# A twelve-stage decoder in float32: a block-sparse ReLU layer by seven block products on token tile pairs, and identity products at places of every stage

## The chip, the cores and the metric

The kernel runs on one core of a Trainium2 chip. The metric is the device time of one execution in microseconds (us), lower is better. Five engines work beside each other, each with its own instruction stream: TensorE (PE in the profile) multiplies matrices and writes to the accumulating memory PSUM, VectorE (DVE), ScalarE (ACT) and GpSimd (POOL) do elementwise work, SyncE (SP) issues the transfers (DMAs). They order themselves by semaphores: an instruction adds to a counter when it has ended, and another engine waits until the counter has reached a number. An engine that waits holds up everything that stands behind the wait in its stream. TensorE's clock has two levels, 2.4 and 1.2 GHz; the profile gives the granted clock of a stretch as a share of the full one (PEclk).

## The reference

The input x has 16 x 64 tokens of 512 numbers, all in float32. Twelve layers follow each other, and each adds to x what it computes from the normalized x: `x = x + layer(layernorm(x), weights)`. The layers are named L0 to L3, each with a part attn, xattn and ffn. The one that is rewritten here is L1's ffn:

```python
inter = xf @ c1_w.T @ c2_w.T                   # 512 -> 16 -> 1792 scores
blk = inter.reshape(tokens, 1792 // 32, 32)
idx = argmax(blk, axis=-1) + arange(0, 1792, 32)   # one of each 32
h = relu(einsum('bkm,bm->bk', w1[idx], xf))    # hidden values of those alone
out = einsum('bk,bkm->bm', h, w2t[idx])
```

The other eleven (gated and attention layers with their own projections, softmaxes and tables) stay as they are in what they compute.

## The kernel before, in words

The 1024 tokens are T = 8 tiles of P = 128; x lies in SBUF throughout, as 128 x 8 x 512. Each layer is a stage with buffers and semaphores of its own (`Stage`, line 66); a barrier of all engines stands between two stages (`begin`, line 90). The stages run in the order l0a, l0x, l0f, l1a, l1x, l1f, l2a, l2x, l2f, l3a, l3x, l3f. Helpers hold what most stages share. `Front` (line 244) normalizes one tile on ACT (`norm`), turns it on TensorE by four products with the identity (`turn`, line 265) and copies it back out of PSUM (`copy`); at the end of a tile ACT copies the result out of PSUM (`out`) and POOL adds it to x (`residual`). `Ahead` measures mean and variance of x for the next stage while this one still runs. `Turned` (line 207, its `turns` at 227) turns all eight tiles at the start of l1x, l3a and l3x.

**l1f** (`stage_l1_ffn`, line 3171) takes one token tile at a time, in a written-out order on each engine. TensorE computes the 16 low values (`lowered`, line 3220), from them the scores of two chunks of 448 (`scores`), the hidden values for all 1792 columns in four chunks of 448 with K = 512 (`chunk`, line 3238), turns the hidden values in 14 blocks of 128 (`hidden_turn`, line 3247), and multiplies them by w2, 14 products of 512 columns (`out`, line 3259). DVE finds the first largest score of each 32 (line 3334 to 3348: largest, equal, times a falling ramp, largest, equal), and then takes the hidden value where it is largest and positive, and 0 elsewhere. ACT copies turned tiles out of PSUM. SP's queue brings the weights in this order: c1, c2, w1 in four column chunks (line 3210), w2. POOL has the additions to x and the roots of the norms alone. The profile counts two records of TensorE for each float32 product and one for each turned block of 128.

**The other places that the diff touches** are single spots of TensorE's streams: ahead of waits, between products, and at ends of stages. In `stage_bias` (l1x), `turns(n, h)` waits for the softmax'd scores before it turns them; `stage_gqa` builds l3a (`rope`) and l3x (`rms`), where `pair_sums` (line 1219) sums squares of queries and `scores` multiplies queries by keys; in `stage_l0_attn` TensorE begins with `context(g, 0)`, `turn(0, 0)` and `gate_up(0)` (24 records, line 2066); in `stage_l0_ffn` a tile's `zg` is turned for its last products (line 2523); `stage_small_attn` builds l1a (with `context`) and l2a; `stage_l2_ffn` has a chain of small steps per tile between TensorE and DVE; `stage_l3_ffn` is the last stage.

Each engine's order is written out by hand in these functions; no planner moves anything.

## Time and profile before

| | |
|---|---|
| time, median of 3 runs | 4074.86 us (4074.83 to 4080.53) |
| profiled execution, its own time | 4081.22 us |
| its span | 4079.4 us |
| TensorE busy / VectorE / ScalarE / GpSimd | 3819.3 / 2447.5 / 1403.4 / 696.3 us |
| mean granted TensorE clock | 0.966 of the full one |
| l1f, TensorE's first to last product | 1883.65 to 2128.9 us of the span |

A group line of the profile reads: line, engine, operation, out <- in, shapes, count | busy us, mean ns of one | idle time of the engine before them, and what ended most of it. A timeline line reads: start, duration, engine, line, work, number of records [idle before it <- what ended it]. A window line gives for a stretch the busy time of PE, PEld (loading of the stationary side, which overlaps PE), DVE, ACT and POOL with the number of instructions, then the granted clock, the DMA engines' share and GB/s.

### The profile page before, as it was taken

How to read it: one execution, taken by the hardware profiler on the slowest of the kernel's cores; microseconds unless marked ns; L12 is line 12 of the kernel's file. 1: busy time of each engine (PE TensorE's matmuls, PEld its weight loads, DVE VectorE, ACT ScalarE, POOL GpSimd, SP SyncE). 2: the span in 40 equal slices, each digit the busy share in tenths (PEclk: the TensorE clock that was granted, in tenths of full speed). 3: DMA queues.
4: the chain of work that ended last, by engine and by line, in shares of the span. 5: the costliest groups of instructions: out<-in, count | busy, mean ns of one | idle time of the engine just before them, and what ended most of it. 6: DMA issues, size and time to landing. Idle time of an engine off the chain costs nothing. (4 is left out here: it accounts for less than half of the span.)

```text
span 4079.4 us, 50937 instructions
## 1 busy us (share of the span) xinstructions
PE 3819.3 (94%) x18954; PEld 2130.2 (52%) x18954; DVE 2447.5 (60%) x4150; ACT 1403.4 (34%) x2522; POOL 696.3 (17%) x680
## 2 busy tenths in 40 slices
PE   8899989998989899999999889799999989999997
PEld 3343435554456477775447664345555545555564
DVE  0988955552247455555447658876766665565563
ACT  2988935552223211111113334211111133333232
POOL 1111111121001344441000111121211110000000
PEclk9999989999989899999999989899999999999998
DMA  5111121001100433311001022101001021111110
GB/s 191 54 37 52 51 72 34 32 29 61 41 35 14 174 114 115 129 53 75 1 29 41 1 105 60 66 2 41 22 21 42 1 69 37 37 37 37 42 37 24
DMA packets 133966, 215.40 MB, mean 53 GB/s; under 512 B 42576, under 2 KB 95056, under 8 KB 123104
## 3 DMA queue, kind: packets, MB, share of 16 engines
q1 hardware_dynamic: 133728, 212.19, 14.9%
q8 instruction: 154, 2.52, 0.2%
q14 instruction: 84, 0.69, 0.1%
HBM read 168.12 MB, written 44.04 MB: 52 GB/s over the span
## 5 line engine op out<-in xcount | busy, mean ns | idle before, releaser
L1320 PE MATMUL l3a_po<-l3a_wo,l3a_cT 128*128 128x512 f32 x512 | 231.2, 600 | 1.2 <-ACT l3a_cT L1517 1.2
L1320 PEld LDWEIGHTS l3a_po<-l3a_wo,l3a_cT 128*128 128x128 f32 x512 | 96.2, 191 | 121.0 <-issue 116.6
L830 DVE TENSOR_TENSOR x<-x,l1x_po 128x512 f32<-128x512 f32 (+1 forms) x154 | 88.3, 581 | 89.0 <-PE l1x_po L622 88.2
L1208 PE MATMUL l3x_pj<-kvT,l3x_ws 128*128 128x512 f32 x256 | 121.6, 607 | 2.3 <-DVE l3x_qT L1647 2.2
L1208 PE MATMUL l3a_pj<-kvT,l3a_ws 128*128 128x512 f32 x256 | 120.7, 605 | 1.5 <-ACT l3a_saves L1459 0.8
L2796 POOL TENSOR_TENSOR l0x_q<-l0x_q,l0x_qi 128x512 f32<-128x512 f32 x64 | 65.3, 1042 | 303.6 <-DVE l0x_qi L3084 303.6
L1320 PE MATMUL l3x_po<-l3x_wo,l3x_cT 128*128 128x512 f32 x256 | 115.3, 593 | 0.7 <-ACT l3x_cT L1517 0.7
L1320 PE MATMUL l3x_pc<-l3x_wo,l3x_cT 128*128 128x512 f32 x256 | 115.2, 593 | 0.0
L1105 POOL TENSOR_TENSOR l3x_ws<-l3x_wq 128x256 f32<-128x256 f32 x16 | 13.8, 860 | 579.5 <-DMA l3x_wo<-in_L_xattn_Wo 377.6
L2349 DVE TENSOR_SCALAR_CACHE_REDUCE l0a_keep<-l0a_keep,l0a_scalars 128x1376 uint16<-128x1376 uint16 x64 | 105.4, 1646 | 3.6 <-DVE l0a_scalars L2355 1.5
L1614 DVE TENSOR_TENSOR l3a_part<-l3a_raw,l3a_sinq 64x512 f32<-64x512 f32 x128 | 102.2, 799 | 4.0
L3267 PE MATMUL l1f_po<-l1f_w,l1f_hT 128*128 128x512 f32 x224 | 101.6, 599 | 1.9 <-ACT l1f_hT L3310 1.9
L3243 PE MATMUL l1f_ph<-l1f_w,l1f_xT 128*128 128x448 f32 x256 | 103.4, 552 | 0.0
L723 ACT COPY l1x_cT<-l1x_pa 128x512 f32<-128x512 f32 x64 | 34.4, 589 | 197.9 <-PE l1x_pa L614 197.9
L2349 DVE TENSOR_SCALAR_CACHE_REDUCE l0a_keep<-l0a_a,l0a_scalars 128x1376 uint16<-128x1376 uint16 x60 | 98.8, 1646 | 3.8 <-DVE l0a_scalars L2355 1.3
L2212 ACT ACTIVATE l0a_signs<-l0a_lowest_a,l0a_scalars 128x1376 uint16<-128x1376 uint16 x68 | 97.9, 1440 | 6.4 <-DVE l0a_lowest_a L2364 5.3
L622 PE MATMUL l1x_po<-l1x_wo,l1x_cT 128*128 128x256 f32 x376 | 97.2, 381 | 1.2 <-issue 1.2
L1459 ACT COPY l3a_saves<-l3a_pj 128x512 f32<-128x512 f32 x48 | 28.0, 582 | 199.1 <-PE l3a_pj L1208 173.0
L2660 DVE COPY l0x_fill_kv<-l0x_fill 128x512 f32<-128x512 f32 x33 | 22.8, 691 | 120.7 <-PE l0x_fill L2646 62.6
L580 PE MATMUL l1x_pj<-l1x_folds,l1x_ws 128*128 128x512 f32 x192 | 93.7, 614 | 1.5 <-DVE l1x_qT L786 1.5
L194 POOL TENSOR_TENSOR norm_rstd<-norm_half,minus_half 128x1 f32<-128x1 f32 x70 | 41.1, 596 | 315.3 <-DVE norm_half L189 315.3
L1208 PE MATMUL l3x_pj<-kvT,l3x_wq 128*128 128x512 f32 x192 | 90.5, 600 | 3.6 <-DVE l3x_qT L1647 2.3
(591 smaller groups left out, 8898.5 us busy)
## 6 DMA issues: line engine op xcount, KB each, us to landing
l1x_kb<-l1x_keys SPq DMA_DIRECT2D x32, 512.0 KB, 4.7
l1x_vb<-l1x_values SPq DMA_DIRECT2D x32, 512.0 KB, 3.4
l1x_keys<-l0a_kv SPq DMA_DIRECT2D x40, 256.0 KB, 2.0
...
```

Of the source, the lines that this page charges most:

```text
L194: self.nc.gpsimd.tensor_tensor(self.rstd[:, t:t + 1], self.half[:, t:t + 1], self.m.minus_half[:, 0:1], ALU.pow).then_inc(self.root_ready, 1)
L580: mm = pe.matmul(pj[:, p if k % 2 else 1 - p, :], weights, stream, start=c == 0 and not more_of_bank, stop=c == 1, skip_group_check=more_o ...
L622: mm = pe.matmul(bank, rows[:, c], cols[:, c], start=opens and c == 0, stop=c == 1, skip_group_check=not opens)
L830: nc.vector.tensor_tensor(dst, dst, src, ALU.add).then_inc(added, 1)
L1208: mm = pe.matmul(pj[:, p if k % 2 else 1 - p, :], weights, stream, start=c == 0, stop=c == 1)
L1320: mm = pe.matmul(outs[t % 2][:, :], cT[:, h, t * P:(t + 1) * P], wo[:, u, h, :], start=h == 0, stop=h == GH - 1)
L1614: nc.vector.tensor_tensor(batches(part[low:low + S, 1, :]), batches(src[high:high + S]), s, ALU.mult).then_inc(link, chain.next())
L2212: ins = nc.scalar.activation(signs[:, :], words, ACT.Sign, bias=at[:, :], scale=-1.0, accum_out=total[:, :])
L2349: nc.vector.tensor_scalar(below, words, found[:, :], 0.0, ALU.is_lt, ALU.add, accum_out=cnt[:, :]).then_inc(link, step.next())
L2796: nc.gpsimd.tensor_tensor(qv, qv, qi[:, c % 2, b, :].unsqueeze(2).to_broadcast([P, XH, XD]), ALU.mult).then_inc(q_done, 1)
L3243: mm = pe.matmul(ph[:, c % 2, 0:CH1], f.xT[:, u, k, :], w1[:, k, c * CH1:(c + 1) * CH1], start=k == 0, stop=k == KC - 1)
L3267: mm = pe.matmul(f.po[:, :], hT[:, j, :], w2[:, j, :], start=j == 0, stop=j == HC1 - 1)
```

## The change

**First**, a helper issues identity products, which write to a PSUM bank that nobody reads at that time, and whose result is not used:

```diff
+def spin(pe, m, bank, count):
+
+    for _ in range(count):
+        pe.matmul(bank[:, 0:P], m.ident[:, :], m.ident[:, :], start=True, stop=True)
 
 
```

It is called in all stages. The number of products that are executed is 426 as the calls and their loops add up: l0a 25, l0x 42, l0f 30, l1a 34, l1x 39, l1f 26, l2a 48, l2x 24, l2f 72, l3a 33, l3x 44, l3f 9. Most calls stand ahead of a wait, some (at the ends of stages) behind the last product. Where such a call stands ahead of a wait for one engine, the other wait, which guards the bank, is moved ahead of it. Four of the places (l0f; l3x; l3a; `closing` of l3a and l3x), and l1a, where the turn of tile 2 is moved behind the turns of tile 0:

```diff
+                    if n >= T - 2:
+                        pe.wait_ge(zT_ready, n + 1)
+                        spin(pe, m, f.pt, 8 if n == T - 2 else 15)
                     pe.wait_ge(zg_ready, n + 2)
-                    pe.wait_ge(f.xT_ready, n + 3 if not last(n) else n + 2)
                     for k in range(KC):
...
+                        if n == 0 and p == 0:
+                            spin(pe, m, po, 20)
                         pe.wait_ge(q_squared, square_q(n, p) + 2)
...
+                    if rope and hn == 2:
+                        spin(pe, m, px[:, 1], 30)
                     if rope:
...
+                    if rms:
+                        pe.wait_ge(pj_copied, unit_v(GROUPS - 1, NV - 1) + 2)
+                        spin(pe, m, pj[:, 0], 14)
                     turns(GROUPS - 1, 3)
                     attend(GROUPS - 1, 0)
                     rest_of_out(GROUPS - 1, 1)
+                    spin(pe, m, px[:, 0], 3)
 
                 over_groups(opening, group, closing)
...
                 def body(n, u):
                     if within(n + 1):
                         project(n + 1, 1 - u)
-                    if within(n + 2):
+                    if within(n + 2) and not (context and n == 0):
...
@@ -4491,8 +5008,19 @@
                         rotate(n + 1)
                     if n == T - 1:
                         product(n)
+                        spin(pe, m, f.pt, 4)
+                    if context and n == 0:
+                        spin(pe, m, f.pt, 9)
                     turns(n, 0)
+                    if n == T - 1:
+                        spin(pe, m, f.pt, 5)
+                    if context and n == 0:
+                        spin(pe, m, f.pt, 5)
                     turns(n, 1)
+                    if context and n == 0:
+                        f.turn(pe, 2)
+                    if n == T - 1:
+                        spin(pe, m, f.pt, 4)
```

In l0a it is one call of 18 ahead of `gate_up(0)`, in l2f 3 in each tile's round and 5 in each round of the next loop:

```diff
+                    spin(pe, m, f.po, 3)
                     pe.wait_ge(f.xT_ready, n + 2)
                     pe.wait_ge(l_read, n + 1)
                     for k in range(KC):
                         mm = pe.matmul(py[:, 0:ZP], f.xT[:, u, k, :], w[:, k, :], start=k == 0, stop=k == KC - 1)
                     mm.then_inc(l_ready, 1)
 
+                spin(pe, m, f.po, 4)
                 f.turn(pe, 0)
+                spin(pe, m, f.po, 4)
                 pe.wait_ge(loaded, 64)
                 over_tiles(pe, body)
```

**Second**, l1f takes token tiles in pairs p of 0 to 3. The up product of a pair and half the columns (j = 2p + q, q the half) is a product of a 2 x 2 block matrix of x (two tiles by two halves of K) and one of w1 (two halves of K by two chunks of 448 columns), and is computed by seven block products in place of eight, from sums of blocks: four sums of x per pair, four of w1 per half once. The down product has 2 x 2 blocks of h (two tiles by two halves of 896) and of w2 (by two halves of 256 columns), with four sums of h per pair and four of w2 once. All these sums are POOL's:

```diff
+                def mix_x(p, i):
+
+                    u = p % 2
+                    one, two, one2, two2 = x_block(u, 0, 0), x_block(u, 0, 1), x_block(u, 1, 0), x_block(u, 1, 1)
+                    if i == 1:
+                        pool.wait_ge(pt_copied, x_at(p, 1) + 2)
+                        if p >= 2:
+                            pool.wait_ge(up_ready, up_at(2 * p - 3, 7) + 1)
+                        nc.gpsimd.tensor_tensor(xs[:, u, 0], one2, two2, ALU.add).then_inc(x_mixed, 1)
+                    elif i == 2:
+                        pool.wait_ge(x_mixed, 4 * p + 2)
+                        nc.gpsimd.tensor_tensor(xs[:, u, 1], xs[:, u, 0], one, ALU.subtract).then_inc(x_mixed, 1)
+                    elif i == 3:
+                        nc.gpsimd.tensor_tensor(xs[:, u, 2], one, one2, ALU.subtract).then_inc(x_mixed, 1)
+                    else:
+                        pool.wait_ge(x_mixed, 4 * p + 3)
+                        nc.gpsimd.tensor_tensor(xs[:, u, 3], two, xs[:, u, 1], ALU.subtract).then_inc(x_mixed, 1)
...
+                def mix_up(q, i):
+
+                    if i == 1:
+                        pool.wait_ge(w1_loaded[2 * q], 16)
+                        pool.wait_ge(w1_loaded[2 * q + 1], 16)
+                        nc.gpsimd.tensor_tensor(w1s[:, q, 0], up_block(q, 0, 1), up_block(q, 0, 0), ALU.subtract).then_inc(up_mixed, 1)
+                    elif i == 2:
+                        pool.wait_ge(up_mixed, 4 * q + 2)
+                        nc.gpsimd.tensor_tensor(w1s[:, q, 1], up_block(q, 1, 1), w1s[:, q, 0], ALU.subtract).then_inc(up_mixed, 1)
+                    elif i == 3:
+                        nc.gpsimd.tensor_tensor(up_block(q, 0, 1), up_block(q, 1, 1), up_block(q, 0, 1), ALU.subtract).then_inc(up_mixed, 1)
+                    else:
+                        pool.wait_ge(up_mixed, 4 * q + 3)
+                        nc.gpsimd.tensor_tensor(w1s[:, q, 2], up_block(q, 1, 0), w1s[:, q, 1], ALU.subtract).then_inc(up_mixed, 1)
+
+                def mix_down():
+
+                    low_, high = down_block(0, 1), down_block(1, 1)
+                    pool.wait_ge(down_loaded, 16)
+                    nc.gpsimd.tensor_tensor(w2s[:, 0], high, low_, ALU.subtract).then_inc(down_mixed, 1)
+                    pool.wait_ge(down_mixed, 2)
+                    nc.gpsimd.tensor_tensor(low_, low_, down_block(0, 0), ALU.subtract).then_inc(down_mixed, 1)
+                    pool.wait_ge(down_mixed, 3)
+                    nc.gpsimd.tensor_tensor(w2s[:, 1], high, low_, ALU.subtract).then_inc(down_mixed, 1)
+                    pool.wait_ge(down_mixed, 4)
+                    nc.gpsimd.tensor_tensor(w2s[:, 2], down_block(1, 0), w2s[:, 1], ALU.subtract).then_inc(down_mixed, 1)
+                def mix_hidden(p):
+
+                    one, two, one2, two2 = h_block(0, 0), h_block(0, 1), h_block(1, 0), h_block(1, 1)
+                    pool.wait_ge(pt_copied, turn_at(2 * p, 1, 1) + 2)
+                    if p:
+                        pool.wait_ge(down_ready, down_at(p - 1, 7) + 1)
+                    nc.gpsimd.tensor_tensor(hs[:, 0], one, one2, ALU.subtract).then_inc(h_mixed, 1)
+                    pool.wait_ge(pt_copied, turn_at(2 * p + 1, 1, 1) + 2)
+                    pool.wait_ge(h_mixed, sum_at(p, 3) + 1)
+                    nc.gpsimd.tensor_tensor(one2, one2, two2, ALU.add).then_inc(h_mixed, 1)
+                    pool.wait_ge(h_mixed, sum_at(p, 1) + 1)
+                    nc.gpsimd.tensor_tensor(hs[:, 1], one2, one, ALU.subtract).then_inc(h_mixed, 1)
+                    pool.wait_ge(pt_copied, turn_at(2 * p + 1, 0, 1) + 2)
+                    pool.wait_ge(h_mixed, sum_at(p, 2) + 1)
+                    nc.gpsimd.tensor_tensor(hs[:, 2], two, hs[:, 1], ALU.subtract).then_inc(h_mixed, 1)
+
                 f.roots(pool)
-                f.residual(pool, ahead)
+                mix_x(0, 1)
+                mix_up(0, 1)
+                mix_x(0, 2)
+                mix_up(0, 2)
+                mix_x(0, 3)
+                mix_up(0, 3)
+                mix_up(0, 4)
+                mix_x(0, 4)
+                mix_up(1, 1)
+                mix_up(1, 2)
+                mix_up(1, 3)
+                mix_up(1, 4)
+                for i in (1, 2, 3, 4):
+                    mix_x(1, i)
+                mix_down()
+                mix_hidden(0)
+                for p in range(1, T // 2):
+                    if p < T // 2 - 1:
+                        for i in (1, 2, 3, 4):
+                            mix_x(p + 1, i)
+                    mix_hidden(p)
+                    for t in (2 * p - 2, 2 * p - 1):
+                        ahead.root(pool, t, t)
+                ahead.root(pool, T - 2, T - 2)
 
             @block.tensor
```

The seven up products of a j are of two products of 448 columns each, and `down(p, k)` is of seven products of 256 columns. Several of the seven end in one PSUM bank, one after another, and are taken out in between: ACT copies the bank to h four times per j (`save`), DVE adds another bank to it (`join`), and the ReLU now reads h from SBUF in place of PSUM:

```diff
+                    bank = ph[:, {1: 0, 2: 1, 3: 2, 4: 0, 5: 0, 6: 0, 7: 2}[k], 0:CH1]
+                    opens = k in (1, 2, 3)
+                    for c in range(2):
+                        mm = pe.matmul(bank, rows[:, c], cols[:, c], start=opens and c == 0, stop=c == 1, skip_group_check=not opens)
+                    mm.then_inc(up_ready, 1)
+
...
+                    bank = {1: po[:, 0, 0:MID], 2: po[:, 1, 0:MID], 3: po[:, 1, MID:D], 4: po[:, 0, 0:MID],
+                            5: po[:, 1, MID:D], 6: po[:, 1, 0:MID], 7: po[:, 0, 0:MID]}[k]
+                    opens = k in (1, 2, 3, 6)
+                    for c in range(HALF):
+                        mm = pe.matmul(bank, rows[:, c], cols[:, c], start=opens and c == 0, stop=c == HALF - 1, skip_group_check=not opens)
+                    mm.then_inc(down_ready, 1)
...
+                def save(j, what):
+
+                    s, c = {"m1": (0, 0), "u2": (0, 1), "u3": (1, 1), "21": (1, 0)}[what]
+                    act.wait_ge(up_ready, up_at(j, {"m1": 1, "u2": 4, "u3": 5, "21": 6}[what]) + 1)
+                    if j >= 2:
+                        act.wait_ge(pt_filled, turn_at(j - 2, s, 1) + 2)
+                    nc.scalar.copy(hidden(j, s, c), ph[:, 0, 0:CH1]).then_inc(saved, 1)
...
+                def join(j, block):
+
+                    s, c = int(block[0]) - 1, int(block[1]) - 1
+                    dve.wait_ge(up_ready, up_at(j, {"11": 2, "22": 3, "12": 7}[block]) + 1)
+                    dve.wait_ge(saved, saved_at(j, {"11": "m1", "22": "u3", "12": "u2"}[block]) + 1)
+                    nc.vector.tensor_tensor(hidden(j, s, c), hidden(j, s, c), ph[:, 2 if c else 1, 0:CH1], ALU.add).then_inc(joined, 1)
+
+                def relu(j, s):
+
+                    dve.wait_ge(joined, join_at(j, "22" if s else "12") + 1)
+                    if s:
+                        dve.wait_ge(saved, saved_at(j, "21") + 1)
+                    dve.wait_ge(link, hit_at(j, s, 1) + 6)
+                    for c in range(2):
+                        nc.vector.scalar_tensor_tensor(hidden(j, s, c), hidden(j, s, c), 0.0, hits[:, s, c, :],
+                                                       ALU.max, ALU.mult).then_inc(h_ready, 1)
+
```

The additions to x are DVE's, from PSUM, five per pair (256 or 512 columns); ACT's copy and POOL's addition of before are gone. `lowered` is computed once per pair, for 256 tokens. TensorE's order is written out for pairs; the even round, and its beginning and end:

```diff
+                def even(j):
+
+                    p = (j - 4) // 2
+                    hidden_turn(j - 2, 0, 0)
+                    up(j, 1)
+                    scores(j, 1)
+                    hidden_turn(j - 2, 0, 1)
+                    down(p, 5)
+                    hidden_turn(j - 2, 1, 0)
+                    up(j, 2)
+                    hidden_turn(j - 2, 1, 1)
+                    up(j, 3)
+                    down(p, 6)
+                    up(j, 4)
+                    scores(j, 0)
+                    up(j, 5)
+                    down(p, 7)
+                    up(j, 6)
+                    up(j, 7)
...
+                spin(pe, m, pt, 5)
+                turn(0, 0)
+                spin(pe, m, po[:, 0], 6)
+                turn(0, 1)
+                spin(pe, m, po[:, 0], 4)
+                lowered(0)
+                spin(pe, m, po[:, 0], 3)
+                scores(0, 1)
+                for k in (1, 2, 3):
+                    up(0, k)
+                scores(0, 0)
+                for k in (4, 5, 6, 7):
+                    up(0, k)
+                up(1, 1)
...
+                for k in (3, 4, 5, 6, 7):
+                    down(p + 1, k)
+                spin(pe, m, pt, 8)
```

The norm and the turn of x, the first-largest search and the order of the loads are as before; one PSUM bank serves all turned blocks and the low values.

## Rows read from the trace of the kernel before

**Rows 1.** The page: the span and each engine's busy time.

```profile
span 4079.4 us, 50937 instructions
PE 3819.3 (94%) x18954; PEld 2130.2 (52%) x18954; DVE 2447.5 (60%) x4150; ACT 1403.4 (34%) x2522; POOL 696.3 (17%) x680
```

**Rows 2.** Windows of l1f: start:end; length, busy us per engine (instructions), PEclk, DMA share, GB/s.

```profile
1884.00:2131.00 247.00, 241.75 (x752) 118.09 (x750) 124.39 (x215) 32.68 (x63) 14.00 (x16) 0.98 0.08 31
1950.00:1980.00 30.00, 29.76 (x96) 14.59 (x94) 15.62 (x27) 4.17 (x8) 1.77 (x2) 1.00 0.00 1
```

**Rows 3.** Timeline of PE over one token tile of l1f: start, duration, work.

```profile
1950.36 1.02 PE L3235 MATMUL l1f_pi<-l1f_wc,l1f_low 16*128 16x448 f32 x4
...
1980.38 1.02 PE L3235 MATMUL l1f_pi<-l1f_wc,l1f_low 16*128 16x448 f32 x4
```

**Rows 4.** Timeline of PE in l1f's first token tile.

```profile
1902.43 3.17 PE L3243 MATMUL l1f_ph<-l1f_w,l1f_xT 128*128 128x448 f32 x8
1905.44 3.60 PE L3267 MATMUL l1f_po<-l1f_w,l1f_hT 128*128 128x512 f32 x8
1908.87 1.04 PE L3256 MATMUL l1f_pt<-ident,l1f_h 128*128 128x128 f32 x8
```

**Rows 5.** Timeline of PE at the end of l1x: products of 256 columns.

```profile
1876.78 1.03 PE L622 MATMUL l1x_po<-l1x_wo,l1x_cT 128*128 128x256 f32 x4
1877.64 1.03 PE L622 MATMUL l1x_pj<-l1x_wos,l1x_cs 128*128 128x256 f32 x4
```

**Rows 6.** Groups by form, POOL, whole span: work count | busy us, mean ns | idle before.

```profile
L476 POOL TENSOR_TENSOR l1x_ws<-l1x_wq 128x256 f32<-128x256 f32 x16 | 11.8, 740 | 0.0
L1108 POOL TENSOR_TENSOR l3x_ws<-l3x_wq 128x256 f32<-128x256 f32 x16 | 20.4, 1274 | 0.0
L482 POOL TENSOR_TENSOR l1x_sbias<-l1x_sbias,l1x_mask 128x2048 f32<-128x2048 f32 x8 | 36.2, 4521 | 8.0 <-DVE l1x_mask L775 8.0
```

**Rows 7.** Line 3210, the loads of l1f's up weights.

```profile
DMA to landing us min/median/max: 6.1/8.6/10.9
```

**Rows 8.** Groups by form, l1f, DVE.

```profile
L3348 DVE TENSOR_TENSOR l1f_hit<-l1f_rank,l1f_first 128x448 f32<-128x448 f32 x32 | 20.0, 625 | 1.1
```

**Rows 9.** Windows of other stages, columns as in rows 2.

```profile
580.00:610.00 30.00, 24.02 (x89) 8.54 (x90) 19.32 (x24) 12.30 (x22) 8.17 (x8) 0.83 0.09 26
1122.00:1150.00 28.00, 20.00 (x44) 8.59 (x42) 6.26 (x26) 3.21 (x8) 2.32 (x3) 0.76 0.03 10
1180.00:1200.00 20.00, 17.18 (x162) 14.56 (x164) 15.94 (x17) 7.87 (x13) 0.00 (x0) 0.66 0.05 14
1320.00:1336.00 16.00, 10.91 (x40) 5.35 (x40) 3.66 (x7) 3.68 (x5) 1.46 (x2) 0.68 0.06 17
1372.00:1388.00 16.00, 14.26 (x84) 9.01 (x84) 5.71 (x10) 3.85 (x7) 0.00 (x0) 0.68 0.20 67
2672.00:2688.00 16.00, 8.83 (x47) 5.38 (x48) 13.46 (x20) 1.80 (x3) 3.12 (x3) 0.68 0.01 1
2131.00:2162.00 31.00, 20.95 (x185) 18.69 (x186) 10.45 (x16) 5.72 (x10) 1.04 (x2) 0.67 0.58 228
2380.00:2416.00 36.00, 28.20 (x107) 23.15 (x107) 10.17 (x38) 14.47 (x26) 6.33 (x15) 0.53 0.74 295
4032.00:4048.00 16.00, 8.51 (x21) 4.52 (x22) 0.22 (x1) 3.41 (x5) 0.00 (x0) 0.57 0.06 18
```

**Rows 10.** Timeline of PE: gaps in l0f and l3a, [idle before it <-releaser].

```profile
1141.99 1.12 PE L2523 MATMUL l0f_pt<-ident,l0f_zg 128*128 128x128 f32 x4 [4.08 <-DVE l0f_zg L2599]
...
2679.17 1.97 PE L1273 MATMUL l3a_pS<-l3a_kT,l3a_qT 128*64 128x64 f32 x32 [8.74 <-DVE l3a_qT L1617]
```

**Rows 11.** Timeline of PE at new places in l0a and l3x.

```profile
41.85 9.47 PE L2066 MATMUL l0a_pg<-l0a_wg,l0a_xT 128*128 128x512 f32 x24 [0.83 <-ACT l0a_xT L270]
...
3298.44 1.06 PE L1230 MATMUL l3x_pc<-l3x_qsq,l3x_ones 128*32 128x512 f32 x8
3299.44 3.84 PE L1156 MATMUL l3x_pj<-l3x_wv,kvT 128*128 128x128 f32 x32
```

577 lines of the change are left out of this document (443 added, 134 removed).

## The prediction

> **What bounds the kernel now.** I read the page first: TensorE is busy 3819.3 of 4079.4 us, no other engine above 60% [rows 1]. So a change pays where it takes away TensorE's work or lets it run at the higher clock. Then the windows of l1f, the stage that is rewritten: over the stage TensorE is busy 241.8 of 247 us, and in a steady tile 29.76 of 30.00 us, beside 15.6 us of VectorE, 4.2 of ScalarE and 1.8 of GpSimd [rows 2]. The timeline shows the same: a tile starts at 1950.36 and the next at 1980.38, 30.0 us of back to back products [rows 3]. l1f is bound by TensorE alone, and eight tiles of it make 240 us. Last come windows in the other stages, where PEclk lies at 0.53 to 0.83 [rows 9]: there TensorE computes at half clock for a part of the time, after gaps in which it waited [rows 10].
>
> **l1f, TensorE's products.** Eight records of 448 columns take 1905.44 - 1902.43 = 3.01 us, 0.376 each; eight of 512 take 1908.87 - 1905.44 = 3.43 us, 0.429 each [rows 4]. Four records of 256 columns take 0.86 us, 0.215 each [rows 5]: half as wide is half as long, so nothing is lost on the narrower down products. A pair of tiles had 64 up records, 24.1 us, and 56 down records, 24.0 us. It gets 7 x 2 x 2 x 2 = 56 up records, 21.1 us, and 7 x 7 x 2 = 98 of 256 columns, 21.1 us. That is 5.9 us per pair, **-23.8 us** in four.
>
> **l1f, what else TensorE gains.** The low product once per pair, and 0.24 us of waits per tile [rows 2] that two PSUM users less could save: about 0.5 us per pair, -2. The stage's clock of 0.98 over 247 us is at most 5 us lost [rows 2], all at its beginning; the 18 identity products there should give back half, -2.4.
>
> **l1f, what the other engines get.** GpSimd's price for a sum of two tiles: 0.74 us for 256 columns, 4.52 for 2048 [rows 6]; on the line between them 896 columns cost 2.1 us and 1792 cost 4.0. A second row has 256 columns at 1.27 us, in l3x, beside a busier VectorE [rows 6]; that is a factor of 1.7 and my upper price. Per pair GpSimd gets 4 x 0.74 + 4 x 2.1 = 11.4 us (19 at the upper price), of a pair's 54 us. VectorE has 31.2 us per pair, gets six joins of 448 columns near 0.63 [rows 8] and five additions, about 38 to 41 us in all. ScalarE loses two copies, gets eight, about 12. None becomes the bound, and the written-out order puts other products between a bank's fill and its next use; cover for a copy of 0.6 us is a product of 1.5 us (4 x 0.376). If that cover were gone, four copies per j over eight j would cost up to 8 x 4 x 0.6 = 19 us. One wait I do see: at j = 4 the scores wait for VectorE's search of the half before, +2.
>
> **The opening of l1f** is where it pays. A load of w1 lands 8.6 us after issue in the median and 10.9 at most [rows 7], so the second slice is there near 1892, and GpSimd's first sum of w1 can't start before. The four sums of w1 and four of x that j = 0 needs take 4 x 2.1 + 4 x 0.74 = 11.4 us, to 1903.5; at the upper price 19 us, to 1911. TensorE, from about 1890 with 28 records of 0.376 = 10.5 us, would be through near 1900.5. So it waits 3 to 11 us, then perhaps again for the sums of the second half (8.4 us more on GpSimd, for 10.5 us of products). Bounds 3 and 14; I take **+7**, nearer to the cheap price since VectorE is no busier here than in l1x. The sums of w2 (4 x 4.0 = 16, or 27 us) end between 1931 and 1955, and are needed near 1947: hidden by the products of j = 1 and 2, at the upper price up to 8 us late.
>
> The Trainium skill's page "SBUF — State Buffer", section "SBUF: two separate sides", says that a VectorE operation with two SBUF inputs and a GpSimd operation that reads SBUF exclude each other for their whole length. By that rule GpSimd's sums wait for VectorE's search and ReLU, and VectorE for the sums; the trace's 1.27 beside 0.74 agrees with it in kind. By the rule VectorE would stand at up to 41 + 11 = 52 us of the pair's 54, still no bound in the steady part.
>
> **At l1f's end** VectorE adds half tiles straight from PSUM where ScalarE's copy and GpSimd's addition stood; the eight identity products take about what this saves. Sum for l1f: -23.8 - 2 - 2.4 + 7 + 2 = **-19** (from -27 to -4).
>
> **The identity products' price.** One is two records of 128 columns: half of a pair of 256-column records is 0.215 us; by the 32 records of 3.84 us [rows 11] it is 0.24. 426 of them are 92 to 102 us, the double at half clock. In a gap they cost nothing: 15 of them are 3.2 us in a gap of 4.08, 30 are 6.5 in 8.74 [rows 10]. At half clock they would be 6.4 and 12.9, and so 2 and 4 us late. Two places have no gap. In l0a 18 products, 3.9 us, stand ahead of records that waited 0.83 us: +3.0. In l3x 20 products, 4.3 us, stand ahead of line 1230, which followed at 3298.44 with no idle time in front of it: +4.3 [rows 11]. With 0.7 at l1f's end, **+8**. In l2f 62 stand beside VectorE's chain of small steps; I cost them at nothing because VectorE sets that pace; uncovered they are 13 us. The moved waits guard banks that are copied long before, and l1a's turn of tile 2, moved behind the turns of tile 0, has a tile's products before it is needed: nothing for both.
>
> **What the clock gives back.** A stretch with a clock share c has lost at most (1 - c) times its length, if TensorE was busy throughout. Six windows within stages (the first six of [rows 9]) lose 5.1, 6.7, 6.8, 5.1, 5.1 and 5.1 us, and three more of the same kind about 3.4 each: 44 us. TensorE is busy 95 of the 126 us in the six, three quarters, so 33 is what can come back: **-33**. The three stage starts (the last of [rows 9]) lose 10.2, 16.9 and 6.9 us, three more 3.4 each, also 44 us. There TensorE waits for loads (DMA share 0.58 and 0.74) and for norms, which no clock makes faster. Bounds 0 and 30 (its busy share of 0.69); I take **-12**.
>
> **The sum.** -19 - 33 - 12 + 8 = -56 against the profiled execution's own 4081.2 us: 4025. That execution lies 6.4 us above the median shown, with one of the three runs beside it and two at 4074.8; I carry that over: 4019, and say 4020. A measurement of this kernel can tell about 0.2%, 8 us, from no change.
>
> **The rivals.**
> - *The sums are in the way* (B). GpSimd's sums at the upper price or worse, and ScalarE's copies between the products of one bank, eat what the seventh product saves: l1f gives nothing, the clock as forecast. 4081.2 - 37 - 6.4 = 4038. For it: 1.27 us, and up(4), up(5), up(6) all in one bank. Against it: TensorE is the only busy engine.
> - *The clock falls elsewhere* (C). Identity products bridge a gap, but what comes after them is as thin as before, and the clock falls in the next gap; they also run at half clock and end late. Clock gain 0, +8 in the way, l1f -19: 4070, less 6.4: 4064. For it: in four of the six windows TensorE is busy 0.55 to 0.80 of the time. Against it: the windows with a clock of 1.00 have gaps as well, only smaller ones.
> - *Everything works* (D). l1f -27, -44 within the stages, -30 at starts, +8: 4081 - 93 - 6.4 = 3982.
> - *Slower* (E). The identity products stand in front of work that was ready: their places are after a semaphore that comes later than I read it, in l2f, l2a, l1a and at ends. With half of the 92 us in the way and no clock returned it is +46 - 19 = +27, 4102; with all of it 4147. It decides from 19 us in the way, a fifth of the products, with no clock gained. Against it: the gaps of 2 to 9 us are in the trace just where the large calls stand.
> - *It doesn't do what it says* (F): TensorE's clock does not respond to such products and they fit all gaps; with B together, 4075, no change.
>
> **The numbers.** Forecast 0.63, B 0.13, C 0.11, D 0.07, E 0.04, F 0.02. The range takes the forecast's own bounds (l1f 8 either way, in-stage clock 11, starts 12 to 18, added as unlike errors: about 25), reaches over B and towards C and D, and leaves out E, F, most of C and part of D: 3994 to 4056. Faster is all but E and F, 0.94; same 0.02, slower 0.04.
>
> **What would show it.** In the changed kernel: l1f's pair period 54 us in place of 60, TensorE busy all through it, with idle time in its first 25 us put down to GpSimd; VectorE near 40 us per pair. The six windows at a PEclk above 0.9. l0a and l3x some 3 and 4 us longer at the two places. Wrong I would be if idle time stands between the up products of a j in the steady part (B), or if the clock of the six windows stays below 0.8 (C).

## The result, and the profile after

The changed kernel takes 4038.3 us (median of 4 runs, 4035.5 to 4046.2) against 4076.3 us (4 runs, 4074.8 to 4080.5): ratio 0.9913, 95% interval 0.9899 to 0.9927. That is 35 to 38 us less, clear of the 0.2% that can be told, inside the range of 3994 to 4056, and some two thirds of the 56 us forecast. The profiled execution is again a late one of its kernel, 4046.2 us, with a mean granted clock of 0.984 in place of 0.966.

The page, span and busy times:

```profile
span 4044.3 us, 52994 instructions
PE 3842.6 (95%) x19910; PEld 2222.6 (55%) x19910; DVE 2504.3 (62%) x4194; ACT 1416.9 (35%) x2542; POOL 770.5 (19%) x716
```

TensorE is busy 23 us longer than in [rows 1] although the span is 35 us shorter: the identity products count as busy. Taken between the first real products of two stages, as the timeline of TensorE gives them, the stages are as follows (us; l3f from the turning of its weights on; the last two columns are experiments told below):

| stage | before | changed | without the two | small sums |
|---|---|---|---|---|
| l0a | 548.3 | 551.8 | 548.7 | 547.7 |
| l0x | 440.6 | 436.9 | 436.9 | 436.9 |
| l0f | 154.7 | 149.7 | 148.9 | 148.9 |
| l1a | 185.9 | 180.5 | 177.3 | 177.4 |
| l1x | 544.0 | 537.7 | 537.7 | 537.7 |
| **l1f** | 251.4 | 242.4 | 242.4 | 232.9 |
| l2a | 186.9 | 185.9 | 180.9 | 180.5 |
| l2x | 63.3 | 61.3 | 61.8 | 62.1 |
| l2f | 235.5 | 231.4 | 228.9 | 228.8 |
| l3a | 647.3 | 647.7 | 647.2 | 646.9 |
| l3x | 759.7 | 759.3 | 756.7 | 756.5 |
| l3f | 51.7 | 49.6 | 49.7 | 49.8 |

l1f gives 9.0 of its 19 us, and the eleven others 26 together.

**The clock.** Windows of the changed kernel (start:end; length, busy us and instructions of PE, PEld, DVE, ACT, POOL, then PEclk, DMA share, GB/s). The first nine stand at or near the work of the nine windows in [rows 9], moved as the stages are (in the same order); then all of l1a and l1f's beginning:

```profile
580.00:610.00 30.00, 27.89 (x152) 13.93 (x149) 22.05 (x27) 12.91 (x24) 8.18 (x8) 1.00 0.12 36
1122.00:1150.00 28.00, 23.24 (x109) 13.94 (x109) 7.29 (x29) 4.22 (x9) 4.33 (x6) 0.98 0.04 13
1170.00:1190.00 20.00, 16.94 (x185) 14.97 (x185) 15.60 (x16) 8.43 (x14) 0.00 (x0) 0.83 0.06 15
1310.00:1326.00 16.00, 13.76 (x91) 8.87 (x86) 6.86 (x13) 4.39 (x6) 3.08 (x4) 1.00 0.06 17
1355.00:1375.00 20.00, 17.89 (x141) 11.23 (x140) 10.76 (x15) 5.17 (x9) 3.80 (x3) 1.00 0.19 65
2640.00:2656.00 16.00, 14.02 (x88) 9.15 (x87) 14.43 (x22) 1.80 (x3) 1.95 (x2) 0.89 0.01 2
2106.00:2137.00 31.00, 25.75 (x264) 24.14 (x266) 10.50 (x17) 5.73 (x10) 1.08 (x2) 0.89 0.57 228
2352.00:2388.00 36.00, 30.23 (x187) 23.22 (x187) 13.31 (x47) 14.66 (x26) 5.69 (x14) 0.95 0.73 296
3997.00:4013.00 16.00, 9.30 (x39) 7.09 (x38) 1.24 (x8) 4.22 (x7) 0.00 (x0) 0.68 0.07 19
1149.00:1329.00 180.00, 168.03 (x1650) 117.47 (x1646) 116.96 (x135) 67.42 (x105) 19.35 (x18) 0.97 0.09 28
1867.00:1920.00 53.00, 42.20 (x143) 20.52 (x142) 45.20 (x45) 11.63 (x21) 40.91 (x21) 0.90 0.36 142
```

Within the stages 0.83, 0.76, 0.66, 0.68, 0.68 and 0.68 have become 1.00, 0.98, 0.83, 1.00, 1.00 and 0.89, and at the stage starts 0.67, 0.53 and 0.57 are 0.89, 0.95 and 0.68. The forecast asked for above 0.9 within the stages: four of six. l1f's beginning is at 0.90, with gaps of its own. A clock share is not yet time: 0.966 over 4079.4 us is 139 us of full clock lost, 0.984 over 4044.3 us is 65, so 74 us of it came back, and the kernel is 35 us shorter, 9 of them by l1f.

**l1f.** Its steady part first, scores of one half at the same place of two successive pairs on TensorE's timeline (start, duration, work):

```profile
1981.24 1.02 PE L3426 MATMUL l1f_pi<-l1f_wc,l1f_low 16*128 16x448 f32 x4
...
2034.02 1.02 PE L3426 MATMUL l1f_pi<-l1f_wc,l1f_low 16*128 16x448 f32 x4
```

A pair takes 2034.02 - 1981.24 = 52.8 us where two tiles took 60.0 [rows 3]; 54 was forecast. VectorE is busy 40.0 us of it, as forecast, and TensorE all of it. Four pairs at this pace would save 29 us. So some 20 us are lost elsewhere in the stage, and the idle gaps in TensorE's timeline (in brackets, with what ended them) say where:

```profile
1881.93 1.25 PE L3426 MATMUL l1f_pi<-l1f_wc,l1f_low 16*128 16x448 f32 x4 [3.26 <-DVE l1f_hits L3743]
1886.93 1.77 PE L3474 MATMUL l1f_ph<-l1f_w,l1f_xs 128*128 128x448 f32 x4 [0.62 <-ACT l1f_h L3672]
...
1913.45 3.36 PE L3474 MATMUL l1f_ph<-l1f_w,l1f_xs 128*128 128x448 f32 x4 [4.92 <-DVE l1f_h L3759]
...
1922.10 1.77 PE L3474 MATMUL l1f_ph<-l1f_w1s,l1f_xs 128*128 128x448 f32 x4 [1.05 <-DVE l1f_h L3759]
...
1966.80 1.02 PE L3426 MATMUL l1f_pi<-l1f_wc,l1f_low 16*128 16x448 f32 x4 [2.05 <-DVE l1f_hits L3743]
```

There are ten gaps of 0.55 us or more between the stage's first scores and its last products, 14.9 us together, eight of them in the first 65 us. The four longest end with VectorE (3.3, 4.9, 1.1 and 2.1 us); the others are 0.55 to 0.62 us each, mostly for ScalarE's copy between two products of one bank, where the written order of the first halves has nothing to put in between. VectorE's groups in l1f (line, operation, count | busy, mean ns | idle before):

```profile
L3751 DVE TENSOR_TENSOR l1f_hits<-l1f_rank,l1f_first 128x448 f32<-128x448 f32 x32 | 35.5, 1110 | 1.1
L3746 DVE TENSOR_TENSOR l1f_rank<-l1f_hits,ramp 128x448 f32<-128x448 f32 x32 | 35.2, 1099 | 1.1
L3743 DVE TENSOR_TENSOR l1f_hits<-l1f_pi,l1f_best 128x448 f32<-128x448 f32 x32 | 20.0, 624 | 1.1
L3759 DVE TENSOR_TENSOR l1f_h<-l1f_h,l1f_ph 128x448 f32<-128x448 f32 x24 | 14.7, 613 | 2.1 <-PE l1f_ph L3474 1.7 <-ACT l1f_h L3672 0.3
```

These four kinds of pass over 448 columns have the same size, and two cost 1.1 us in place of 0.62 in [rows 8]. They are the two whose inputs both lie in SBUF: the other two read PSUM as well. The ReLU (L3768) has both inputs in SBUF too, and stays at 0.65 us in the mean and 1.15 at most: in this run it hardly ever falls beside a sum. Their single instructions on the timeline of VectorE:

```profile
1904.12 4.45 DVE L3746 TENSOR_TENSOR l1f_rank<-l1f_hits,ramp 128x448 f32<-128x448 f32 x1
1908.61 0.62 DVE L3749 TENSOR_REDUCE l1f_first<-l1f_rank 128x14 f32<-128x448 f32 x1
1909.26 3.61 DVE L3751 TENSOR_TENSOR l1f_hits<-l1f_rank,l1f_first 128x448 f32<-128x448 f32 x1
...
1914.63 2.55 DVE L3746 TENSOR_TENSOR l1f_rank<-l1f_hits,ramp 128x448 f32<-128x448 f32 x1
```

and at the same time on GpSimd's, the sums of w2:

```profile
1904.13 3.96 POOL L3346 TENSOR_TENSOR l1f_w2s<-l1f_w 128x1792 f32<-128x1792 f32 x1
1908.17 4.22 POOL L3348 TENSOR_TENSOR l1f_w<-l1f_w 128x1792 f32<-128x1792 f32 x1
1912.47 4.23 POOL L3350 TENSOR_TENSOR l1f_w2s<-l1f_w 128x1792 f32<-128x1792 f32 x1
```

The rank of 1904.12 ends at 1908.57, 0.5 us after the sum that began at 1904.13 has ended at 1908.09; the mark of 1909.26 ends at 1912.87, again 0.5 us after the next sum. So each step looks as if it waited for a whole sum; whether it does, and with which inputs, is tested below. Over the four sums of w2 VectorE's four ranks and marks took some 12 us more than their 0.62 each, and TensorE stood behind it.

### The profile page after: what moved, and what is told of

Its sections match the earlier page's. It is cut to its first block and busy times, and to the rows that moved or that the text cites. A ratio compares the mean times of both kernels' runs of the same rounds, so it can differ in the third digit from the quotient of the medians.

```text
span 4044.3 us, 52994 instructions
## 1 busy us (share of the span) xinstructions
PE 3842.6 (95%) x19910; PEld 2222.6 (55%) x19910; DVE 2504.3 (62%) x4194; ACT 1416.9 (35%) x2542; POOL 770.5 (19%) x716
## 5 line engine op out<-in xcount | busy, mean ns | idle before, releaser
L2234 ACT ACTIVATE l0a_signs<-l0a_a,l0a_scalars 128x1376 uint16<-128x1376 uint16 x64 | 92.5, 1445 | 1.1
L1220 PE MATMUL l3a_pj<-kvT,l3a_wq 128*128 128x512 f32 x192 | 88.4, 596 | 4.2 <-DMA l3a_wo<-in_L_attn_Wo 2.2
```

The costliest lines, as they stand in the source:

```text
L1220: mm = pe.matmul(pj[:, p if k % 2 else 1 - p, :], weights, stream, start=c == 0, stop=c == 1)
L2234: ins = nc.scalar.activation(signs[:, :], words, ACT.Sign, bias=at[:, :], scale=-1.0, accum_out=total[:, :])
```

## The experiments

All runs are compared with the kernel before, run beside them on the same chip; "less" and "more" of a stage are read from the timelines as in the table.

**The two parts, one at a time.** The first run leaves all identity products out:

```diff
 def spin(pe, m, bank, count):
-    for _ in range(count):
-        pe.matmul(bank[:, 0:P], m.ident[:, :], m.ident[:, :], start=True, stop=True)
+    return
```

> The changed kernel with every identity product left out, so that only the seven-product l1f and the moved waits are new. The theory (two parts that add up): in the changed kernel's trace l1f is 9.0 us shorter from its first product to the next stage's, with its own identity products at the start worth about 2 of that; so 7 us less than before, about 4069 us (4065 to 4072), the mean clock back at 0.966, and VectorE's marks and ranks in l1f again up to 4.4 us long in place of 0.62. Rival (l1f gives its forecast 19 us once no identity product stands in its way): 4057.

Measured: 4071.7 us, ratio 0.9987 (0.9977 to 0.9997). l1f takes 248.1 us, 3.3 less than before and not 7. Two windows of its beginning, and two gaps on TensorE's timeline:

```profile
1880.00:1920.00 40.00, 33.30 (x92) 14.82 (x92) 28.90 (x41) 8.49 (x16) 25.78 (x18) 0.83 0.49 191
1920.00:1970.00 50.00, 42.23 (x138) 22.85 (x137) 39.16 (x44) 10.93 (x20) 27.45 (x11) 0.86 0.00 0
```

```profile
1933.44 2.33 PE L3473 MATMUL l1f_ph<-l1f_w1s,l1f_xs 128*128 128x448 f32 x4 [3.81 <-DVE l1f_h L3758]
1941.45 1.86 PE L3425 MATMUL l1f_pi<-l1f_wc,l1f_low 16*128 16x448 f32 x4 [2.72 <-DVE l1f_hits L3742]
```

The waits of 3.8 and 2.7 us are the same kind as above, and the clock is at 0.83 and 0.86 over 90 us. l1f is 5.7 us longer than with its own identity products, not the 2.4 of the forecast. One more stage moved here: l1x takes 539.6 us with no identity product in it, 4.4 less than before. Whether its moved wait or chance in the clock does that is open. The second run has l1f of before (its function put back as it was) and everything else of the change:

```diff
 def stage_l1_ffn(nc, m, w_c1, w_c2, w_1, w_2):
-    HALF, MID = HC1 // 2, D // 2
...
+        f = Front(nc, st, m)
```

> The old l1f beside all identity products of the other stages. The theory: the eleven other stages are 27 us shorter in the changed kernel's trace (spans between first products of the stages), so 4076 - 27 = 4049 us (4045 to 4053), mean clock about 0.983. Rival (the new l1f's dense products are what keeps the clock for the stages behind it): l2a and l2x lose 3 us or more, 4053 or above.

Measured: 4047.7 us, ratio 0.9940 (0.9924 to 0.9957). So by the ratios the identity products of the other stages bring 24 us, the new l1f alone 5, and the whole change 35, each known to within 4 to 7 us. The 6 us between are what the identity products in l1f itself bring there (242.4 us against 248.1), but the intervals alone would allow for none. l2a and l2x lose nothing (179.6 and 61.6 us); the rival falls. l1f takes 253.6 us, 2.2 more than before, with its code unchanged; no run shows why.

**The two places in the way:**

```diff
-                spin(pe, m, f.po, 18)
                 gate_up(0)
...
-                        if n == 0 and p == 0:
-                            spin(pe, m, po, 20)
                         pe.wait_ge(q_squared, square_q(n, p) + 2)
```

> The changed kernel without the 18 identity products ahead of gate_up(0) in l0a and the 20 ahead of the first pair_sums in l3x. The theory (they stand in front of work that was ready and give no clock back): l0a 3.5 us and l3x 4 us shorter, 4031 us (4028 to 4034) against 4038. Rival (they keep the clock high in what follows): a stretch at half clock appears behind one of the two places and the time is 4036 or more.

Measured: 4029.9 us, ratio 0.9890 (0.9873 to 0.9906) against 0.9913 (0.9899 to 0.9927); the intervals overlap, and the two stages have to decide. In the changed kernel they stood as two runs of records on TensorE:

```profile
40.78 4.18 PE L60 MATMUL l0a_po<-ident 128*128 128x128 f32 x36
...
3264.88 4.73 PE L60 MATMUL l3x_po<-ident 128*128 128x128 f32 x40
3269.54 1.06 PE L1244 MATMUL l3x_pc<-l3x_qsq,l3x_ones 128*32 128x512 f32 x8
```

4.2 and 4.7 us long, and line 1244 follows at once. Without them the first one's place shows

```profile
42.09 9.47 PE L2084 MATMUL l0a_pg<-l0a_wg,l0a_xT 128*128 128x512 f32 x24 [0.85 <-ACT l0a_xT L277]
```

a gap of 0.85 us, as before. l0a is 3.1 us shorter and l3x 2.6, 5.7 of the 8 us by the medians, and no new stretch at half clock appears behind either. Over all profiles l3x takes 759.3 to 760.6 us with these products and 756.3 to 758.3 without, l0a 549.3 to 552.0 and 546.6 to 548.7, so the two costs hold. The two profiles differ by 17 us, and most of the rest looks like chance: l1a, whose code is the same in both, is 3.2 us shorter, l2a 5.0 and l2f 2.5. For l1a

```profile
1145.00:1322.00 177.00, 165.02 (x1650) 114.58 (x1646) 117.11 (x135) 67.14 (x105) 19.29 (x18) 0.99 0.09 29
```

the clock is 0.99 where the changed kernel's trace has 0.97 over the same work; in all eleven other profiles with identity products it took 177.3 to 177.5 us. The changed kernel's own profile caught the clock low there and in l2a; together these are 8 us, as much as it lies above its median.

**Turns in place of products:**

```diff
-    for _ in range(count):
-        pe.matmul(bank[:, 0:P], m.ident[:, :], m.ident[:, :], start=True, stop=True)
+    for _ in range(2 * count):
+        pe.transpose(bank[:, 0:P], m.ident[:, :], m.ident[:, :])
```

> Each identity product is replaced by two turns of the identity in TensorE's transpose mode, so about the same time on TensorE and the same places. Theory one (any occupation of TensorE holds its clock): mean clock 0.984, 4038 us (4034 to 4042). Theory two (the Trainium skill, page TensorE: Matmul & The Clock Gate, Part 4: PE-mode transpose, says that a transpose does not count as busy in the same way): the mean clock falls back to near 0.966 while the time in the way stays, 4065 us or more.

Measured: 4045.6 us, ratio 0.9926 (0.9910 to 0.9943), not to be told from the change's 0.9913. The clock and two windows:

```profile
core 0: 4046.0 us, clock 0.984
```

```profile
580.00:610.00 30.00, 27.65 (x151) 13.21 (x146) 21.72 (x27) 12.57 (x22) 8.17 (x8) 1.00 0.12 36
2640.00:2656.00 16.00, 13.87 (x94) 9.67 (x93) 14.50 (x22) 1.80 (x3) 2.88 (x3) 0.89 0.01 2
```

0.984, and 1.00 and 0.89 in the windows, as with real products, and most stages take what they take with products (l0x 436.9, l1a 177.3, l2x 61.3 us). So in these stages a float32 turn in transpose mode holds the clock as a product does, and theory two falls; the time lies somewhat above the 4034 to 4042 us of theory one. The exception is l1f: it takes 250.6 us, 8 more than in the change, at a granted clock of 0.94, as low as in the run without any identity product and not 0.97. Whether the turns or chance did that is open.

**GpSimd's sums and VectorE.** First, the twelve sums of weight blocks are left out, and then the four of w2 alone. Of the first:

```diff
-                        nc.gpsimd.tensor_tensor(w1s[:, q, 0], up_block(q, 0, 1), up_block(q, 0, 0), ALU.subtract).then_inc(up_mixed, 1)
+                        nc.gpsimd.tensor_tensor(thin[:, 4 * q + 0:4 * q + 1], m.ident[:, 0:1], m.ident[:, 0:1], ALU.subtract).then_inc(up_mixed, 1)
...
-                        rows, cols = xs[:, u, 0], w1s[:, q, 0]
+                        rows, cols = xs[:, u, 0], up_block(q, 0, 0)
```

> The changed kernel, but GpSimd's sums of weight blocks (eight of w1, four of w2) are left out: in their place it adds one column each, with the same semaphores, and TensorE reads plain blocks of the same size, so the output is not the reference's. The theory (these sums hold VectorE's operations with two SBUF inputs back, and VectorE holds TensorE): VectorE's marks and ranks fall to 0.62 us near l1f's start, the idle time of TensorE in front of up products and scores there (3.3, 4.9, 1.1 us and more) goes but for the copies' 0.6 each, and l1f is 10 to 14 us shorter: 4026 us (4022 to 4031). Rival (the opening is bound by the loads and by ScalarE's copies between products of one bank): at most 4 us shorter, 4034 or above.

and of the second, which changes w2's sums and their readers alone:

```diff
-                    nc.gpsimd.tensor_tensor(w2s[:, 0], high, low_, ALU.subtract).then_inc(down_mixed, 1)
+                    nc.gpsimd.tensor_tensor(thin[:, 0:1], m.ident[:, 0:1], m.ident[:, 0:1], ALU.subtract).then_inc(down_mixed, 1)
...
-                        rows, cols = hs[:, 1], w2s[:, 1]
+                        rows, cols = hs[:, 1], down_block(0, 0)
```

> The same for the four sums of w2 alone; the eight of w1 stay. The theory: TensorE's 4.9 and 1.1 us in front of products at 1913 and 1922 us, while VectorE's rank and mark took 4.4 and 3.6 us beside sums of 4 us each, go: l1f 5 to 7 us shorter, 4032 us (4029 to 4036). Rival (what counts are the sums of w1 in the opening, the later ones are hidden): 4037 or above.

Measured: 4022.1 us, ratio 0.9870 (0.9854 to 0.9887), with l1f at 227.8 us, 14.6 less; and 4029.0 us, ratio 0.9888 (0.9869 to 0.9907), with l1f at 234.4, 8.0 less. So the sums cost l1f 14.6 us, 8.0 of them those of w2, which the prediction had hidden. TensorE's gaps without any weight sum:

```profile
1874.06 1.02 PE L3428 MATMUL l1f_pi<-l1f_wc,l1f_low 16*128 16x448 f32 x4 [0.81 <-DVE l1f_hits L3745]
1877.40 1.77 PE L3476 MATMUL l1f_ph<-l1f_w,l1f_xs 128*128 128x448 f32 x4 [0.62 <-ACT l1f_h L3674]
...
1948.44 1.02 PE L3428 MATMUL l1f_pi<-l1f_wc,l1f_low 16*128 16x448 f32 x4 [2.05 <-DVE l1f_hits L3745]
```

The wait of 3.3 us is 0.8, the copies' 0.6 are still there and so is the one of 2 us at j = 4; those of 4.9 and 1.1 us are gone. All gaps that are left in l1f come to 5.9 us: 2.1 at j = 4, the rest ScalarE's copies and 0.8 for VectorE.

The gaps of 14.9 us have become 5.9, which is 9.0 of the 14.6. The rest is the clock. Windows over l1f of the changed kernel, without w2's sums, and without any weight sum:

```profile
1866.00:2108.00 242.00, 225.25 (x917) 146.69 (x916) 180.30 (x265) 45.41 (x85) 88.27 (x53) 0.97 0.08 32
1858.00:2092.00 234.00, 223.68 (x917) 145.63 (x916) 169.00 (x265) 45.31 (x85) 72.33 (x54) 0.98 0.09 34
1861.00:2089.00 228.00, 220.28 (x922) 145.04 (x922) 160.63 (x265) 45.65 (x85) 56.36 (x54) 1.00 0.09 36
```

0.97, 0.98 and 1.00: by these shares some 7, 5 and 0 us are lost to the clock. w2's sums cost 6.4 us of gaps (8.5 are left without them) and some 2 of clock; w1's cost 2.6 us of gaps and some 5 of clock, which falls behind the gap of 3.4 us in front of the second scores.

That shows that the sums do it, not how. The next run leaves all sums in place, and takes away the second SBUF input of VectorE's steps:

```diff
-                    nc.vector.tensor_tensor(blocks(mask), score, best[:, :].unsqueeze(2).to_broadcast(wide),
+                    nc.vector.tensor_tensor(score, score, best[:, :].unsqueeze(2).to_broadcast(wide),
                                             ALU.is_equal).then_inc(link, 1)
                     dve.wait_ge(link, done + 3)
-                    nc.vector.tensor_tensor(blocks(rank[:, :]), blocks(mask), m.ramp[:, :].unsqueeze(1).to_broadcast(wide),
+                    nc.vector.tensor_tensor(score, score, m.ramp[:, :].unsqueeze(1).to_broadcast(wide),
                                             ALU.mult).then_inc(link, 1)
...
-                        pe.wait_ge(link, hit_at(j, 1, 1) + 3)
+                        pe.wait_ge(link, hit_at(j, 1, 1) + 6)
```

> The changed kernel, but VectorE keeps marks and ranks of the search in the scores' own PSUM bank, so that none of its five steps has two SBUF inputs; the next scores of TensorE wait for the whole search and not for its first two steps. GpSimd's sums are all there. The theory (an exclusive lock between a VectorE operation with two SBUF inputs and a GpSimd operation, not a shared bandwidth): VectorE's five steps take 0.62 us each also beside the sums, l1f is 4 to 9 us shorter, 4031 us (4028 to 4035); the longer wait for the scores gives some of it back in the steady part. Rival (any VectorE operation is slowed by GpSimd's sums, or the other way): steps of more than 1 us stay, no gain, 4038 or above.

Measured: 4045.0 us, ratio 0.9928 (0.9912 to 0.9945): no gain. But the step itself (durations in ns, least/median/most, of 32):

```profile
L3745 DVE TENSOR_TENSOR l1f_pi<-l1f_pi,ramp x32: 632/632/633, 1867.4 to 2071.5; 128x448 f32<-128x448 f32 x32
```

never takes more than 633 ns, beside all the same sums of up to 4.2 us. What waits now is the ReLU, whose inputs are both in SBUF; on VectorE's timeline

```profile
1904.58 0.63 DVE L3745 TENSOR_TENSOR l1f_pi<-l1f_pi,ramp 128x448 f32<-128x448 f32 x1
...
1906.98 8.27 DVE L3767 SCALAR_TENSOR_TENSOR l1f_h<-l1f_h,l1f_hits 128x448 f32<-128x448 f32 x2
```

two of them take 8.3 us in place of 1.15, one sum of w2 each. And the longer wait that the edit adds for the next scores shows on TensorE:

```profile
1919.11 1.86 PE L3425 MATMUL l1f_pi<-l1f_wc,l1f_low 16*128 16x448 f32 x4 [6.63 <-DVE l1f_hits L3750]
...
1964.68 1.02 PE L3425 MATMUL l1f_pi<-l1f_wc,l1f_low 16*128 16x448 f32 x4 [4.06 <-DVE l1f_hits L3750]
```

6.6 and 4.1 us. GpSimd is freed as well: its 256-column sums of x take 1.1 us in seven of 16 cases in the changed kernel and 0.73 in 14 of 16 here. So the steps came out as the theory has it and not as the rival, while the time came out as the rival's: the cure is not one. l1f takes 250.7 us, 8 more, 3.5 of them gaps and most of the rest clock (0.95 in place of 0.97). The same with the first scores moved and without the two places:

```diff
-                for k in (1, 2, 3):
+                for k in (1, 2, 3, 4, 5):
                     up(0, k)
                 scores(0, 0)
-                for k in (4, 5, 6, 7):
+                for k in (6, 7):
                     up(0, k)
```

> Both: marks and ranks in PSUM, the first scores(0, 0) moved behind up(0, 5), and without the identity products ahead of gate_up(0) in l0a and of the first pair_sums in l3x. The theory: gains of the two add up, 8 and 7 us: 4022 us (4018 to 4027). Rival (l1f's beginning is bound by the sums themselves once VectorE is free): l1f only 4 us shorter, 4027 to 4031.

Measured: 4037.2 us, ratio 0.9914 (0.9895 to 0.9933), outside the forecast and its rival. That is 8 us below the run before, about what the two places are worth, and l1f is no better (249.9 us).

If one waits for the other's whole instruction, then short instructions are the cure:

```diff
+                def sums(n, dst, a, b, op, sem):
+                    for c in range(n):
+                        last_ = nc.gpsimd.tensor_tensor(dst[:, c], a[:, c], b[:, c], op)
+                    last_.then_inc(sem, 1)
...
-                        nc.gpsimd.tensor_tensor(w1s[:, q, 0], up_block(q, 0, 1), up_block(q, 0, 0), ALU.subtract).then_inc(up_mixed, 1)
+                        sums(2, w1s[:, q, 0], up_block(q, 0, 1), up_block(q, 0, 0), ALU.subtract, up_mixed)
...
-                    nc.gpsimd.tensor_tensor(w2s[:, 0], high, low_, ALU.subtract).then_inc(down_mixed, 1)
+                    sums(HALF, w2s[:, 0], high, low_, ALU.subtract, down_mixed)
```

> The kernel without the two (e3_without_two), and GpSimd makes each sum of w1 in two pieces of 448 columns and each of w2 in seven of 256. More instructions on GpSimd, about 5.2 in place of 4.2 us per sum of w2, but each holds VectorE's operations back for 0.7 to 1.2 us at most in place of 2.1 to 4.2. The theory (an operation waits for the other engine's running one to end, so its length is what hurts): no mark or rank of VectorE longer than 1.9 us, l1f 3 to 7 us shorter than in e3_without_two (242.4), 4025 us (4021 to 4029). Rival (GpSimd takes the port again between its pieces before VectorE gets it): marks and ranks of 4 us stay, no gain, 4030 or more.

Measured: 4018.2 us (4017.5 to 4020.3), below the 4021 to 4029 expected; ratio 0.9856 (0.9839 to 0.9872), clear of the change's, and just clear of the 0.9890 (0.9873 to 0.9906) without the two. The ranks and the marks:

```profile
L3748 DVE TENSOR_TENSOR l1f_rank<-l1f_hits,ramp x32: 624/626/2494, 1867.4 to 2053.8; 128x448 f32<-128x448 f32 x32
L3753 DVE TENSOR_TENSOR l1f_hits<-l1f_rank,l1f_first x32: 624/626/1736, 1869.6 to 2055.1; 128x448 f32<-128x448 f32 x32
```

The longest is 2.5 us (beside a hidden sum, which stays whole) in place of 4.4; the expectation had 1.9. Beside the pieces of w2's sums no step takes more than 1.2 us. l1f is 232.9 us, 9.5 less, and over all of it

```profile
1859.00:2091.00 232.00, 221.18 (x913) 145.12 (x912) 171.02 (x262) 45.22 (x84) 99.43 (x86) 0.99 0.09 34
```

the clock is 0.99 in place of 0.97: TensorE's gaps come to 9.0 us in place of 14.9, and the clock falls only once behind them. GpSimd works 99 us here in place of 89, and that shows nowhere in the time.

The w2 sums on VectorE instead, one each behind `relu(1, 0)`, `join(2, "22")`, `join(2, "12")` and `relu(2, 1)`:

```diff
+                relu(1, 0)
+                mix_down(0)
                 join(2, "22")
+                mix_down(1)
                 hit(2, 1, 0)
                 join(2, "12")
+                mix_down(2)
```

> The kernel without the two, and the four sums of w2 are VectorE's, one each behind relu(1, 0), join(2, 22), join(2, 12) and relu(2, 1). The theory: VectorE spends 4 x 1.9 = 7.7 us on them, where it stood 12 us in wait for GpSimd's, and can place them where TensorE isn't waiting for it: l1f 3 to 6 us shorter, 4026 us (4022 to 4030). Rival (VectorE is the bound there in any case): 4030 or more.

Measured: 4032.3 us, ratio 0.9890 (0.9873 to 0.9906), l1f 242.4 us: nothing gained, the rival's time. Each sum takes 2.0 us, but the last one comes late in VectorE's order, and down(0, 2) waits for it:

```profile
1934.68 5.74 PE L3507 MATMUL l1f_po<-l1f_w2s,l1f_hT 128*128 128x256 f32 x13 [6.96 <-DVE l1f_w2s L3781]
```

So it is this order that fails, and not yet the idea; a better order wasn't tried.

**How many identity products.** Half of each count, on the kernel without the two:

```diff
-    for _ in range(count):
+    for _ in range((count + 1) // 2):
```

> The kernel without the two, with half of each remaining count of identity products (rounded up). The theory (they must fill their gaps to hold the clock): half of what the clock gave back is lost: mean clock 0.975 to 0.98, 4045 us (4038 to 4052). Rival (few products are enough): clock 0.985, 4030 us or less, since less stands in the way.

Measured: 4033.8 us, ratio 0.9890 (0.9873 to 0.9906), the same as with all, clock 0.982 in place of 0.987. Both the 4038 to 4052 of the theory and the 4030 of the rival were missed. Eleven stages keep what they had within about 2 us. The exception is l2f, 7.4 us longer; its window with half the products, and then with all:

```profile
2343.00:2579.00 236.00, 210.81 (x619) 109.83 (x618) 182.61 (x567) 88.53 (x166) 28.86 (x34) 0.93 0.24 81
```

```profile
2345.00:2574.00 229.00, 208.53 (x673) 108.86 (x672) 182.34 (x567) 88.41 (x166) 28.59 (x33) 0.97 0.25 83
```

0.93 against 0.97 (0.89 before, at the same 236 us). There a chain of short steps between TensorE and VectorE leaves many small gaps, and the full counts are needed. With half of them the clock share rose from 0.89 to 0.93 and the stage gained nothing; why the time came only with the other half is open. So the expected loss came in one stage alone, and the others seem to have more products than they need.

The last run joins what had helped: small sums, half the counts but in l2f, and one order:

```diff
                     up(j, 1)
-                    scores(j, 1)
+                    if j > 4:
+                        scores(j, 1)
                     hidden_turn(j - 2, 0, 1)
                     down(p, 5)
+                    if j == 4:
+                        scores(j, 1)
```

> The kernel with small sums (e9_small_sums), with half of each count of identity products but in l2f, where the full counts stay, and with scores(4, 1) of l1f behind down(0, 5), where TensorE waited 2.06 us for VectorE in every run so far. The theory: l2f's length returns to about 229 us (236.2 with half the products), since its chain of short steps is where the clock needs them; the wait of 2 us in l1f goes; the rest as with half the products: 4014 us (4009 to 4018). Rival (the phase of the clock decides from run to run, and halved counts let it fall in other places): 4018 to 4024. Second rival for l1f: the 2 us come back as a wait for a later search.

Measured: 4016.6 us (4015.0 to 4019.4), ratio 0.9850 (0.9834 to 0.9867). l2f is 228.7 us, as expected, and l1f 228.3, 4.6 less than with small sums where 2 were expected; the 2 us of waiting at j = 4 are gone without coming back. In l1f's opening TensorE now waits four times, 4.9 us together, for GpSimd's sums of w1 themselves, which is the wait that the prediction had there. l2a, l3a and l3x are 2.4, 0.7 and 1.8 us longer than with small sums alone, at a lower clock. So it beats both kernels, by 61 us and 22 us, but not, for certain, the kernel with small sums.

## Why the prediction was right in sign, and short in size

- **TensorE's products in l1f (-23.8) and the low product (-2)**: right, and a little better: 52.8 us per pair, -29 in four.
- **The opening (+7)**: right in size by luck, as the sums of w1 cost 14.6 - 8.0 = 6.6 us. The way was another: the sums are in time for TensorE in the changed kernel, and it is VectorE that they hold; and only 2.6 us are waits, the rest is the clock that falls behind one of them, which the sum didn't have.
- **The wait at j = 4 (+2)**: right, 2.1 us, and gone in the last run.
- **The sums of w2 ("hidden by the products of j = 1 and 2")**: this step failed. They are ready at 1921 us, long before they are needed, and still cost 8.0 us, since VectorE's search stands for them and TensorE's banks for VectorE. The prediction had weighed the exclusion of the two engines only as busy time in the steady part (52 of 54 us), and there TensorE has no gap. It should have been weighed where one sum is 4 us long and VectorE is a link of the chain.
- **ScalarE's copies ("cover for a copy of 0.6 us is a product of 1.5 us")**: the cover is not there in the first halves; some 3 us.
- **Sum of l1f**: -29 + 6.6 + 8.0 + 5.9 (all other gaps) = -8.5, measured -9.0. The -29 is the steady pace taken for all four pairs, so the agreement is better than the working. The clock in it (-2.4 for its identity products) was too small a term: with all of them out l1f is 5.7 us longer.
- **The two places in the way (+7.3)**: right in kind, 5.7 us in the two stages.
- **The clock in the other stages (-33 - 12)**: the eleven stages gave 26 us in the profile, with the two places in it, so about 32 came back of 45, 35 by the medians. l0x, l0f, l1a and l1x gave 3.6, 5.0, 5.4 and 6.4 us, though 4.4 of l1x's 6.4 came without any identity product. l3a gave nothing, though 5.1 us of its loss stood in the sum: VectorE ends its wait of 8.7 us [rows 10], and the identity products (6.9 us, and 2.0 of idle time behind them) only fill it. The share of three quarters was too high for windows in which another engine sets the end. Over the whole kernel, l1f and the two places included, the time that came back is 35 of 74 us of lost clock, under a half.
- **Rivals**: B (the sums are in the way) held in part: the weights' sums took 14.6 us of what l1f would have gained, and by way of VectorE. C fell: the clock rose to 0.984. The 24 us of the other stages rule out F, in which they are nothing, and D, in which they are over 60. E did not come.
